# Graph network on one core: one-hots read column numbers from PSUM, and GpSimd gathers every tile of three sums

## The reference, cut to what matters

```python
x = _layernorm(x + _L0_gnn_ref(x, edge_weight1, ...))             # two relational sums
x = _layernorm(x + _L1_gnn_ref(x, edge_index, edge_weight, ...))  # one graph convolution
x = _layernorm(x + _L2_gnn_ref(x, edge_index, ...))               # two attention layers
x = _layernorm(x + _L3_gnn_ref(x, node_vec1, src, dst, ...))      # tensor product convolution
```

```python
msg = Hr[src, etype] * norm                            # relational, twice (table of 32 rows per node)
agg = jax.ops.segment_sum(msg, dst, num_segments=N)
weighted = h[src] * edge_weight[:, None]               # graph convolution
aggregated = jax.ops.segment_sum(weighted, tgt, num_segments=num_nodes)
in_deg = jax.ops.segment_sum(edge_weight, tgt, num_segments=num_nodes)
```

## Time and profile before

| | |
|---|---|
| median of 3 runs | 9353.69 us |
| span of the profiled execution | 11372.5 us |
| mean granted TensorE clock | 0.683 |
| busy: POOL (GpSimd) | 6601.0 us, 58% |
| busy: PE (TensorE) | 7449.0 us, 65% |
| busy: DVE (VectorE) | 5876.2 us, 52% |
| busy: ACT (ScalarE) | 3125.7 us, 27% |

### The profile page before, as it was taken

How to read it: one execution, slowest core, us unless ns; L and a number is a source line. 1 busy time by engine, 2 the same in 40 slices (tenths; PEclk the granted TensorE clock), 3 DMA queues, 4 the chain that set the end, 5 groups by cost and what they waited for, 6 DMA issues and landing times. The chain is left out here.

```text
span 11372.5 us, 179298 instructions
## 1 busy us (share of the span) xinstructions
PE 7449.0 (65%) x38061; PEld 5413.9 (48%) x38181; DVE 5876.2 (52%) x20918; ACT 3125.7 (27%) x10511; POOL 6601.0 (58%) x6970
## 2 busy tenths in 40 slices
PE   5444445555584555567878677777577777788888
PEld 3222223333333333333333366666465566777777
DVE  5555543333333333345544466666566666677776
ACT  2111110000020000000000144444344444677776
POOL 3666666666615666656666566666466665455554
PEclk5555557666696666667776665555666656899999
DMA  4222223111151111111111111111111111211111
GB/s 99 70 70 68 69 74 81 45 46 46 46 228 45 46 46 46 45 46 46 45 46 45 45 49 49 48 48 48 43 49 48 48 48 40 77 41 41 41 41 40
DMA packets 312751, 637.84 MB, mean 56 GB/s; under 512 B 138402, under 2 KB 181541, under 8 KB 300200
## 3 DMA queue, kind: packets, MB, share of 16 engines
q0 software_dynamic: 222080, 416.54, 14.1%
q1 hardware_dynamic: 81444, 212.40, 5.5%
q10 hardware_dynamic: 8484, 1.48, 0.1%
HBM read 479.02 MB, written 150.90 MB: 55 GB/s over the span
## 5 line engine op out<-in xcount | busy, mean ns | idle before, releaser
L1188 POOL DMA_INDIRECT relsum_rows<-relation_table,tab_idx x1950 | 1846.7, 947 | 1328.5 <-issue 452.2
L1246 PE MATMUL relsum_sums<-relsum_hot,relsum_rows 128*128 128x128 f32 x3900 | 1127.6, 385 | 1242.4 <-issue 668.2
L1246 PEld LDWEIGHTS relsum_sums<-relsum_hot,relsum_rows 128*128 128x128 f32 x3900 | 1014.3, 280 | 1678.9 <-issue 1497.8
L1053 POOL DMA_INDIRECT conv_rows<-tensor_table,src_idx x997 | 942.7, 946 | 754.9 <-PE conv_sums L2367 361.3
L1053 POOL DMA_INDIRECT gat2sum_rows<-gat_table,src_idx x997 | 945.1, 948 | 589.9 <-PE gat2sum_sums L1978 301.3
L1053 POOL DMA_INDIRECT gat1sum_rows<-gat_table,src_idx x997 | 945.3, 948 | 587.5 <-PE gat1sum_sums L1978 276.3
L717 POOL DMA_INDIRECT records<-sort_recs,place_rows x968 | 929.7, 960 | 602.0 <-DVE place_rows L235 339.2
L1188 POOL DMA_INDIRECT gcnsum_rows<-x_table,src_idx x985 | 937.4, 952 | 572.5 <-issue 230.2
L1249 PE MATMUL relsum_streamed<-relsum_wide 128*128 128x512 bf16 x1874 | 996.1, 532 | 0.0
L1976 PE MATMUL gat1sum_sums<-gat1sum_hot,gat1sum_scaled 128*128 128x128 f32 x1994 | 695.6, 449 | 399.6 <-DVE gat1sum_scaled L1905 327.6
L1976 PE MATMUL gat2sum_sums<-gat2sum_hot,gat2sum_scaled 128*128 128x128 f32 x1994 | 670.9, 436 | 423.2 <-DVE gat2sum_scaled L1905 291.3
(11 more groups left out here) (416 smaller groups left out, 17092.5 us busy)
## 6 DMA issues: line engine op xcount, KB each, us to landing
relation_table<-table_row SPq DMA_DIRECT2D x30, 2048.0 KB, 6.3
relsum_rows_SP<-relation_table SPq DMA_DIRECT2D x2816, 0.5 KB
relsum_rows_ACT<-relation_table ACTq DMA_DIRECT2D x2816, 0.5 KB
relation_table<-sort_space SPq DMA_DIRECT2D x40, 1024.0 KB
relsum_rows<-relation_table,tab_idx POOLq DMA_INDIRECT x1950
place_lo_wide<-lo_rows SPq DMA_DIRECT2D x121, 256.0 KB
gcnsum_rows_SP<-x_table SPq DMA_DIRECT2D x1536, 0.5 KB
relation_table<-place_extra SPq DMA_DIRECT2D x20, 1024.0 KB
```

The source lines that it names most:

```text
L1053: pool.indirect_dma_start(bufs[:, t % depth, :], None, table, bass.IndirectOffsetOnAxis(ap=idx[:, t:t + 1], axis=0)).then_inc(landed[t % l ...
L1188: pool.indirect_dma_start(rows[:, t % depth, :], None, table, bass.IndirectOffsetOnAxis(ap=idx[:, t:t + 1], axis=0)).then_inc(landed[t % d ...
L1246: pe.matmul(bank[:, 0:P], tile_rows, hot[:, t % HOTS, :], start=True, stop=True).then_inc(s["multiplied"], 1)
```

## The change

The one-hots of the three sums read the column numbers from a PSUM bank. At the start of each sum VectorE copies `env.iota_row` into it. `RowByRow`, its lists, its DMAs and the `aside` lists are gone; GpSimd gathers all 997 tiles. To free a bank, two pairs of uses that had a bank each now share one (`small_ps` and `turn_ps` in `relsum1`, `flag_ps` and `turn_ps` in `gcnsum`), with one wait for each on the last transposed x having been copied out.

```diff
+    def digits(self, ps):
+        return ps("digits", [P, 512], F32)[:, 0:P]
...
-    LISTS_AT = 5 * PIECES
...
-        self.small_ps = ps("small", [P, 512], F32)
+        self.small_ps = self.turn_ps
...
         if t == self.WEIGHTS_AT:
             pe.wait_ge(s["small_in"], 16 * self.small_loads)
+            pe.wait_ge(s["x_kept"], -(-NPAD // 512))
...
-class RowByRow:
...
-        numbers = sb("numbers", [64, max(count for _, _, count in aside) * P], I32)
-        by_row = {kind: RowByRow(env, tag, kind, first, count, idx, table, sb, numbers) for kind, first, count in aside}
-        side_of = {t: r for r in by_row.values() for t in r.tiles}
+        digits = beside.digits(ps)
...
         def _(sp):
             beside.sync(sp)
-            if "SP" in by_row:
-                by_row["SP"].program(sp, s["multiplied"], v["multiplied"])
...
                 beside.pool_at(pool, t)
-                if t in side_of:
-                    continue
                 if t >= depth:
...
             beside.act(act)
-            if "ACT" in by_row:
-                by_row["ACT"].program(act, s["multiplied"], v["multiplied"])
...
             def build(t):
-                dve.tensor_scalar(hot[:, t % HOTS, :], env.iota_row[:, :], env.dst_rel[:, t:t + 1], weight[:, t:t + 1],
+                dve.tensor_scalar(hot[:, t % HOTS, :], digits, env.dst_rel[:, t:t + 1], weight[:, t:t + 1],
                                   ALU.is_equal, ALU.mult).then_inc(s["hot_ready"], 1)
 
+            dve.tensor_copy(digits, env.iota_row[:, :])
             beside.clear(dve, acc)
...
-                if t in side_of:
-                    pe.wait_ge(*side_of[t].landed_at(t))
-                    tile_rows = side_of[t].buffer(t)
-                else:
-                    pe.wait_ge(landed[t % depth].sem, landed[t % depth].at(16 * gathered(t)))
-                    tile_rows = rows[:, t % depth, :]
+                pe.wait_ge(landed[t % depth].sem, landed[t % depth].at(16 * (t // depth + 1)))
...
-        self.flag_ps = ps("flags_turn", [P, 512], F32)
         self.turn_ps = ps("x_turn", [P, 512], F32)
+        self.flag_ps = self.turn_ps
...
+            if g == 0:
+                pe.wait_ge(s["x_kept"], len(self.quads()))
```

More of the change, by code:

```diff
@@ L19 @@
 I32 = mybir.dt.int32
-U8 = mybir.dt.uint8
 ALU = mybir.AluOpType
@@ L24 @@
 DVE_ENGINE = mybir.EngineType.DVE
-ENGINES = {"SP": mybir.EngineType.SP, "ACT": mybir.EngineType.Activation}
 P = 128
@@ L738, in pool_at @@
         pass
-    LISTS_AT = -1
     def pe_first(self, pe):
@@ L1138, in sum_over_slots @@
-def sum_over_slots(env, tag, idx, table, weight, acc, aside, degree=False, beside=None, banks=BANKS, stream=0):
+def sum_over_slots(env, tag, idx, table, weight, acc, degree=False, beside=None, banks=BANKS, stream=0):
     nc = env.nc
@@ L1158, in sum_over_slots @@
         beside.memory(sb, ps)
-        numbers = sb("numbers", [64, max(count for _, _, count in aside) * P], I32)
-        by_row = {kind: RowByRow(env, tag, kind, first, count, idx, table, sb, numbers) for kind, first, count in aside}
-        side_of = {t: r for r in by_row.values() for t in r.tiles}
+        digits = beside.digits(ps)
         groups = range(-(-USED // SLOT_BUFS))
-        def gathered(t):
-            return len([u for u in range(t % depth, t + 1, depth) if u not in side_of])
         block = ctx.enter_context(nc.Block(no_gpsimd_drain=True))
@@ L1199, in build @@
             def build(t):
-                dve.tensor_scalar(hot[:, t % HOTS, :], env.iota_row[:, :], env.dst_rel[:, t:t + 1], weight[:, t:t + 1],
+                dve.tensor_scalar(hot[:, t % HOTS, :], digits, env.dst_rel[:, t:t + 1], weight[:, t:t + 1],
                                   ALU.is_equal, ALU.mult).then_inc(s["hot_ready"], 1)
+            dve.tensor_copy(digits, env.iota_row[:, :])
             beside.clear(dve, acc)
-            if beside.LISTS_AT < 0:
-                for side in by_row.values():
-                    side.make_list(dve)
             if degree:
@@ L1225, in _ @@
                     beside.dve_at(dve, t)
-                    if t == beside.LISTS_AT:
-                        for side in by_row.values():
-                            side.make_list(dve)
         @block.tensor
@@ L1245, in _ @@
                     pe.matmul(bank[0:1, P:2 * P], env.ones[:, 0:1], hot[:, t % HOTS, :], start=True, stop=True)
-                pe.matmul(bank[:, 0:P], tile_rows, hot[:, t % HOTS, :], start=True,
+                pe.matmul(bank[:, 0:P], rows[:, t % depth, :], hot[:, t % HOTS, :], start=True,
                           stop=True).then_inc(s["multiplied"], 1)
@@ L1253, in sum_over_slots @@
         for k in range(depth):
-            landed[k].passed(16 * len([t for t in range(k, USED, depth) if t not in side_of]))
+            landed[k].passed(16 * len(range(k, USED, depth)))
 def unit_blocks(u):
@@ L1512, in relational_layer @@
         prepare = ReloadAndPrepare(env, inp, records, weights_dram[REL:2 * REL, :], weights, acc)
-        sum_over_slots(env, "relsum1", env.tab_idx, table, env.w1, acc1, beside=prepare, banks=4, stream=512,
-                       aside=(("SP", 222, 10), ("ACT", 262, 10)))
+        sum_over_slots(env, "relsum1", env.tab_idx, table, env.w1, acc1, beside=prepare, banks=4, stream=512)
         second_table(env, weights, table, acc1[:, 0, :], inp["L0_gnn_bias1"])
@@ L1519, in clear @@
             pass
-    sum_over_slots(env, "relsum2", env.tab_idx, table, env.w1, acc[:, 0:1, :], beside=FromX(), stream=512,
-                   aside=(("SP", 63, 12), ("ACT", 103, 12)))
+    sum_over_slots(env, "relsum2", env.tab_idx, table, env.w1, acc[:, 0:1, :], beside=FromX(), stream=512)
     finish_layer(env, "relout", RelationalEnd(env, acc), x_table)
@@ L1661, in gcn_layer @@
     sum_over_slots(env, "gcnsum", env.src_idx, x_in, env.w, acc, degree=True, beside=GraphSum(env, flags, acc),
-                   banks=5, stream=256, aside=(("SP", 79, 12),))
+                   banks=5, stream=256)
     finish_layer(env, "gcnout", GraphEnd(env, acc), table, env.gat_w[0], TABLE_WIDTH)
```

46 lines of the change are left out of this document (removed).

## The result

The changed kernel takes **9418.5 us** (median of 4 runs, 9417.2 to 9419.0); before, run beside it, took 9355.0 (9352.2 to 9357.8). The ratio is 1.0067 with a 95% interval of 1.0055 to 1.0079: 63.5 us, or 0.7%, slower. The prediction was 9405 with a range of 9367 to 9432, and a chance of 0.85 for slower.

The account below looks back on a forecast made before the run. GpSimd's step per gather was taken to bound the kernel. 29.9 + 35.8 - 22 + 17.9 + 0.9 = +62.5 us on the profiled 11372.5 us, scaled by 0.8225 to +51.4, gave 9405 us, range 9367 to 9432.

Parts of the forecast that it names:

- What bounds it: Whole kernel: GpSimd issues gather after gather, and its step of at most 1.243 us bounds the time.
- Part 1: Three sums: GpSimd gets 20, 24 and 12 more gathers, costing +29.9, +35.8 and +17.9 us on the profiled execution.
- Part 2: Second sum: waits behind SyncE's side tiles go, giving back 22 us, between 14.9 and 35.4.
- The other leg of the term: Second sum against first: a gather costs 1.516 us against 1.493, and 972 x 0.023 = 22 us.
- Part 3: Three sums: one-hots from PSUM take 400 ns instead of 341, hidden beside GpSimd; gathers gain 0, at most about 3 us.
- Part 4: Copies to PSUM and the new bank waits: 0.9 us for three copies, the rest nothing.
- The sum: Whole kernel: +62.5 us on the profiled execution, scaled to +51.4 us on the runs, so 9405 us.
- nothing given back: Second sum: the case where removing the side fetch saves no wait, the forecast's own upper end of 9426 us.
- First rival: Gathers beside one-hots in the three sums get faster, 72 us back, 9333 us; deciding from 17 ns a gather; chance 0.08.
- Second rival: Second sum: the side fetch paced it before, so removing it gives 9364 us, within or near 0.2%; chance 0.09.
- Third rival: Third sum: VectorE becomes the bound; at 22 us per 16 tiles 124 us more, 9529 us; chance 0.03.
- scaling of 0.8225: Whole kernel: median of the runs, 9353.7 us, over the profiled span, 11372.5; it turned +62.5 us into +51.4.

Follow-up runs that it names:

- the halves: Changed kernel with one-hots from SBUF: 9443.8 us against 9371.6 for before; kernel before with one-hots from PSUM, side fetch kept: 9365.9 against the same 9371.6.
- ordinary profile of before: The kernel before, unchanged, profiled once more: 9359.7 us in its one run, span 9357.8 us, against 11372.5 us in its first profiled execution.
- The last run: The changed kernel, unchanged, run again in a comparison slowed by the 2 us pauses: 11293.1 us against 11326.2 for before, ratio 0.9974.

## Why the prediction was right, and where it was not

- **What bounds it**: right. GpSimd's step is the price of everything: 20 and 30 gathers fewer and 56 more came out within some 2 us of 1.25 us each in the halves and in the kernels with more side tiles. The bound of "at most 1.243 us" was 5 to 9 ns low: the 783 us that it leaves outside the gathers came from the stretched execution; the same sum over the ordinary profile of before gives 714 us, and then 1.254 us with the scatters in it.
- **Part 1, 56 gathers more**: right without pauses, 69.6 us predicted and 56 x 1.25 = 70 shown. The 1.49 us of the earlier trace rows is the price only where the pauses are.
- **Part 2, -22 us given back**: this is the term that failed. The ordinary profile of before has no wait at tile 63, GpSimd loses 0.9 us behind SyncE's tiles in the second sum, and the true term is about 0 where the prediction gave back 22 us, outside its bounds of 14.9 to 35.4. The step that failed is the reading of a wait out of a stretched execution: the prediction had said itself that it was stretched by pauses, took them out of the gather's step, and left them in the wait. A wait for SyncE was not free of them: its row costs 0.918 us in the earlier trace rows and 0.40 in an ordinary run. The other leg of the term failed as well: it compared the second sum with the first, where the side fetch runs too. The last run is nearer to the right comparison for those conditions, the same sum without the fetch: the second sum's step is 75 ns shorter there, 73 us over 972 gathers where the prediction took 22, though from profiles of two comparisons and with the one-hots changed as well.
- **Part 3, one-hots**: 404 ns for 400, hidden, as predicted; VectorE never became the bound, nor in the second sum with a copy of 417 ns more per tile. That the gathers gain nothing was wrong by some 5.5 us, by one comparison up to 10 (bound: 3). Two things hid it. The median, 947 ns, is blind to a minority of lengthened gathers. And the attention passes are no measure of a gather undisturbed by VectorE: their gathers average 948 ns for 947 in the relational sums, with maxima of 1089 and 1058 for 1027 and 1022. The same sum without the one-hots in SBUF is the measure, and there the maxima fall to 994 and 961.
- **Part 4**: nothing shown against it.
- **The sum**: 70 - 0 - 5.5 + 0.9 = 65, measured 63.5 and 64.3. The prediction's 51 came from -18 where 0 was true, and 0 where -5.5 was; that the second error took back a third of the first is luck. The measured time lies in the range because its upper end was set for "nothing given back", which is what happened (that case adds up to 9424, not 9426).
- **First rival** (the gathers get faster): its mechanism exists and is worth 2 ns, far from the 17 at which it would decide. **Second rival** (side fetch paced the sums): refuted for the runs, where SyncE waits for TensorE; in the stretched execution, where SyncE waits for no buffer in the second sum, it comes nearest to the truth. **Third rival** (VectorE the bound): refuted, the third sum's step is 1.252 us.
- The sign holds for runs without the pauses, the 9355 us of the metric. With them the change is 0.26% faster, a case that the prediction's scaling of 0.8225 had wrongly merged with the first.

## What to carry to other kernels

Look first whether the profiled execution is a run like the timed ones. Where its span is 20% longer, no wait of it may go into the sum, only durations that agree with the runs; a second profile costs less than such a term. Where one engine's step paces a stage, every instruction moved off it to another queue is worth the whole step, as long as that queue keeps up: here that paid from 56 side tiles to 86, without the pauses; with them taking all 56 back was faster. And when the question is whether something is sometimes held up, ask for the mean and the maximum of a group, not the median, and compare with the same stage without the suspect, not with another stage.

## What the runs showed that was not expected

- A VectorE copy of 417 ns within SBUF beside each gather lengthens GpSimd's step by 92 ns; one of 415 ns from PSUM by nothing. Smaller ones within SBUF cost 12 ns (256 columns) and 43 ns (two of 128); a one-hot of 342 ns within SBUF costs 2.
- On some comparisons all runs are 20% longer (11,211 and 11,326 us instead of 9355), with pauses of 2 us in GpSimd's timeline. VectorE and TensorE stand in them too: after the pause of the earlier trace rows VectorE starts again at 2498.81 us, GpSimd at 2499.05, TensorE at 2499.25. In the untouched convolution a gather's step is 1.60 us then, against 1.26. What causes them stays open. These two comparisons ran on two chips, the experiments with ordinary times on two others, so the chip may be what differs.
- A weak hint: they got rarer in the three sums, and there alone, with the change, and one of the DMA queues in the page of the profile, the one that brings instructions, moves less in the changed kernel. But it moves the same, 579 transfers before and 431 after, in the profiles that have no pauses, so its amount alone doesn't make them. The queue's row (transfers, MB, share of 16 engines) in the kernel before and then in the changed one:

```profile
q14 instruction: 579, 4.74, 0.1%
```

```profile
q14 instruction: 431, 3.52, 0.1%
```

- Under those conditions the same change has the other sign: 0.7% slower without the pauses, 0.3% faster with them.
